# Attention scores over 128 contraction rows, and attention values with both split parts side by side, in one kernel

## The reference

```
xn = layernorm(x); q = (xn @ w_q) / 8; k, v = split(context @ w_kv)
scores = einsum('bqhd,bkhd->bhqk', q, k)          # 112 x 375 for each head
attn = softmax(scores, axis=-1)
out = einsum('bhqk,bkhd->bqhd', attn, v).reshape(B, SQ, 1024) @ w_out + b_out
x = x + tanh(g) * tanh(gate) * out
# then: Fourier mix, a one-head attention, a mixture of 16 experts (top 4), each with a layernorm ahead
```

## Time and profile before

| | |
|---|---|
| median of 3 runs | 1162.66 us (1161.47 to 1164.37) |
| the profiled execution | 1161.57 us |
| its span | 1159.8 us |
| outside the span | 1.8 us |
| PE busy | 1075.9 us, 93% |
| DVE busy | 773.1 us, 67% |
| ACT busy | 631.4 us, 54% |
| POOL busy | 519.8 us, 45% |
| mean granted TensorE clock | 0.984 |
| bytes moved by DMA | 95.8 MB |

### The profile page before, as it was taken

One profiled execution on the slowest core, in us unless ns is written; L12 is line 12 of the kernel. 1 busy time (PEld: TensorE's weight loads), 2 busy tenths in 40 slices (PEclk: granted clock), 3 DMA queues, 4 the chain that ended last, 5 costly groups with the idle time before them and its releaser, 6 DMA issues.

```text
span 1159.8 us, 22342 instructions
## 1 busy us (share of the span) xinstructions
PE 1075.9 (93%) x7361; PEld 930.8 (80%) x7361; DVE 773.1 (67%) x1963; ACT 631.4 (54%) x1676; POOL 519.8 (45%) x745
## 2 busy tenths in 40 slices
PE   3889999999999999999999999999999779899995
PEld 3688888888888888888788888888887668789983
DVE  2544677767676767776676777676766665686665
ACT  2533556555656565655556565656564545555650
POOL 3512345453535454454535354536354404565441
PEclk9989999999999999999999999999999888999998
DMA  5395882010101011010001010101000522234469
GB/s 150 96 329 207 309 297 63 5 34 9 30 27 31 27 31 35 23 35 22 23 16 32 8 38 9 31 9 31 5 18 9 176 83 78 99 108 152 133 198 287
DMA packets 82382, 95.82 MB, mean 83 GB/s; under 512 B 9291, under 2 KB 74445, under 8 KB 82272
## 3 DMA queue, kind: packets, MB, share of 16 engines
q1 hardware_dynamic: 41904, 44.94, 13.5%
q10 hardware_dynamic: 31520, 32.51, 7.9%
q0 software_dynamic: 8848, 16.96, 4.2%
HBM read 41.98 MB, written 52.39 MB: 81 GB/s over the span
## 4 chain that ended last, share of the span: by engine, by line
PE 61%; DVE 16%; ACT 10%; issue 6%; DMA 4%; POOL 3%; SPq 1%; DVEq 0%; ACTq 0%; POOLq 0%
PE ps_kv L1568 14%; PE ps_ot L1854 8%; PE ps_ot L1668 5%; PE ps_kv L1650 5%; PE ps_s L1811 5%; PE ps_pt L1821 5%; ACT prob L938 4%; DVE negmax L1467 3%; PE ps_pt L1780 3%; PE ps_ot L1793 3%; DVE pT_lo L1478 2%; DVE k_lo L1152 2%; ACT v_hi L928 2%; DMA zb<-places 2%; PE ps_ot L1712 2%
## 5 line engine op out<-in xcount | busy, mean ns | idle before, releaser
L855 POOL TENSOR_TENSOR prob<-prob,rinv 112x750 f32<-112x750 f32 x128 | 185.4, 1448 | 310.7 <-DVE rinv L1472 310.4
L938 ACT ACTIVATE prob<-ps_s,negmax 112x375 f32<-112x375 f32 x256 | 144.7, 570 | 236.4 <-DVE negmax L1467 236.4
L1478 DVE TENSOR_TENSOR pT_lo<-ps_pt,pT_hi 125x672 fp32r<-125x672 f32 x128 | 109.7, 857 | 77.0 <-ACT pT_hi L1051 77.0
L1568 PE MATMUL ps_kv<-ctxT_hi,wkv 128*128 128x376 f32 x512 | 141.6, 357 | 7.8 <-DVE v_lo L1156 3.8
L1467 DVE TENSOR_REDUCE negmax<-ps_s 112x2 f32<-112x750 f32 x128 | 119.0, 930 | 0.1
L1156 DVE TENSOR_TENSOR v_lo<-ps_kv,v_hi 125x512 fp32r<-125x512 f32 x96 | 66.4, 692 | 77.2 <-ACT v_hi L928 77.2
L1568 PE MATMUL ps_kv<-wkv,ctxT_hi 128*125 128x512 f32 x384 | 112.2, 414 | 3.6 <-DVE n_e L1116 2.3
L1821 PE MATMUL ps_pt<-ident,prob 112*125 112x112 f32 x768 | 104.9, 273 | 1.3 <-POOL prob L855 1.3
L814 POOL DMA_INDIRECT places<-ysb,place_i x72 | 70.3, 976 | 69.1 <-ACT ysb L1010 55.9
L1051 ACT ACTIVATE pT_hi<-ps_pt 125x672 fp32r<-125x672 f32 x128 | 93.5, 730 | 9.0 <-PE ps_pt L1821 1.0
L1821 PEld LDWEIGHTS ps_pt<-ident,prob 112*125 112x125 f32 x768 | 95.1, 191 | 1.7 <-POOL prob L855 1.7
(11 more groups left out here) (298 smaller groups left out, 2623.8 us busy)
## 6 DMA issues: line engine op xcount, KB each, us to landing
rows_by_expert<-stage_w ACTq DMA_DIRECT2D x16, 1920.0 KB, 7.3
xg<-rows_by_expert SPq DMA_DIRECT2D x72, 128.0 KB, 2.1
zb<-places SPq DMA_DIRECT2D x16, 448.0 KB, 15.0
arena<-in_L_ffn_mlp_w SPq DMA_DIRECT2D x24, 256.0 KB, 4.4
ctx_in<-in_ctx SPq DMA_DIRECT2D x16, 375.0 KB
acc<-in_L_xattn_w_kv SPq DMA_DIRECT2D x4, 512.0 KB, 13.1
stage_w<-in_L_ffn_mlp_w SPq DMA_DIRECT2D x8, 256.0 KB, 3.0
x_in<-in_x SPq DMA_DIRECT2D x16, 112.0 KB, 2.1
```

Source lines behind the costliest of these rows:

```text
L855: e_prob.done(eng.tensor_tensor(prob[0:TQ, p % 2, :, :], prob[0:TQ, p % 2, :, :], rinv[:, 2 * p:2 * p + 2].unsqueeze(2).broadcast_to([TQ, ...
L938: e_exp.done(eng.activation(prob[0:TQ, p % 2, half, :], S[0:TQ, half, 0:SK], ACT.Exp, bias=negmax[:, h:h + 1], accum_out=rowsum[:, h:h + 1]))
L1478: e_pt_lo.done(eng.tensor_tensor(pT_lo[:, :, :, :].rearrange("p h k t -> p h (k t)"), PT[0:KEYT, :, 0:NKEY * TQ], pT_hi[:, :, :, :].bitcas ...
L1568: last = eng.matmul(out_, lhs(i, k), rhs(j, k), start=(n == 1), stop=(n == KT * len(PASSES)))
```

## The change

Nothing else of the computation is changed; the three terms are the same.

- **Scores.** `kx` holds for each head hi keys on partitions 0 to 63 and lo keys on 64 to 127. `qx_hi` holds hi queries twice, on both halves; `qx_lo` holds lo queries on 0 to 63 and zeros on 64 to 127. S(p) is then four matmuls over 128 rows. ACT writes a pair's hi keys in two copies instead of one (the second moves head 1 from partitions 64 to 127 down to 0 to 63). DVE writes the lo keys to `k_low`, the lo queries to `q_nat`, and SP moves them into place with DMAs between two SBUF places: two for each pair's keys, six for each half of the queries, 28 a batch. S(p) waits for these DMAs instead of for DVE.
- **Values.** `vx` holds hi and lo values of one head side by side (128 columns), `pT` hi and lo probabilities side by side (224 columns). O(p) is six matmuls of 125x128 by 125x224, whose four quarters are the four products, of which lo x lo is not used. The three others are added outside PE: ACT copies one (64x224, `o_part`), DVE adds a second to it (64x224), waits for that, and adds the third in two instructions of 64x112 that write `oT`. These three are on DVE after `pT_lo` in every odd slot.
- **Order.** `KV_AT`: k2, v2 from slots 0, 1 to 1, 2; x from 10 to 9; c0, c1 from 12, 13 to 11, 12; q0 from 14 to 12; k0, k1 from 14, 15 to 13, 14. SP's loads are written by slot between the moves.
- **Room.** `acc` is gone, its uses go to `stage_w`; `TURN`, the order in which experts' weights are placed, and the filling with zeros follow from that.

```diff
-        KV_AT = (("k", 2, 0), ("v", 2, 1), ("k", 3, 3), ("q", 1, 4), ("k", 4, 5), ("v", 3, 6),
-                 ("k", 5, 7), ("v", 4, 8), ("k", 6, 9), ("v", 5, 10), ("k", 7, 11), ("x", 0, -6),
-                 ("c", 0, -4), ("c", 1, -3), ("q", 0, -2), ("k", 0, -2), ("k", 1, -1), ("v", 0, -1),
+        KV_AT = (("k", 2, 1), ("v", 2, 2), ("k", 3, 3), ("q", 1, 4), ("k", 4, 5), ("v", 3, 6),
+                 ("k", 5, 7), ("v", 4, 8), ("k", 6, 9), ("v", 5, 10), ("k", 7, 11), ("x", 0, -7),
+                 ("c", 0, -5), ("c", 1, -4), ("q", 0, -4), ("k", 0, -3), ("k", 1, -2), ("v", 0, -1),
                  ("v", 1, 0), ("r", 0, 36), ("e", 0, 38))
...
+                if kind == "k":
+                    for head in range(2):
+                        eng.dma_start(kx[64:128, n, head, :].bitcast(F32),
+                                      k_low[64 * head:64 * head + 64, n % 2, :].bitcast(F32)
+                                      ).then_inc(f_k[n % 2], 16)
...
-                        for half in range(2):
-                            rows_ = slice(64 * half, 64 * half + 64)
-                            last = eng.activation(oT[rows_, p, :], OT[rows_, half * TQ:(half + 1) * TQ],
-                                                  ACT.Copy)
-                        e_oT.done(last)
+                        e_part.done(eng.activation(o_part[:, :, :], O[64:128, :, 0, :], ACT.Copy))
...
-                    ins = eng.activation(k_hi[:, n, :], bank[:, 0:SKE], ACT.Copy)
+                    eng.activation(kx[:, n, 0, :], bank[:, 0:SKE], ACT.Copy)
+                    ins = eng.activation(kx[0:64, n, 1, :], bank[64:128, 0:SKE], ACT.Copy)
...
+                for p in range(NP):
+                    st = due(g, AT_O[p] + 1)
+                    if st:
+                        e_part.wait_ge(eng, st, p + 1)
+                        co(eng.tensor_tensor(o_part[:, :, :], O[0:64, :, 1, :], o_part[:, :, :], ALU.add))
+                        co.wait_ge()
+                        for half in range(2):
+                            last = eng.tensor_tensor(oT[64 * half:64 * half + 64, p, :], O[0:64, half, 0, :],
+                                                     o_part[:, half, :], ALU.add)
+                        e_oT.done(last)
...
-                        eng.wait_ge(kv_dve, KV_LO[max(use_of(st, "q", p // 4), use_of(st, "k", p)) + 1])
+                        eng.wait_ge(f_q, queries(st.off, p // 4) + Q_MOVES)
+                        eng.wait_ge(f_k[p % 2], keys(st.off, p) + K_MOVES)
                         e_exp.wait_ge(eng, st, 2 * p)
-                        for n, (i, j) in enumerate(PASSES):
-                            for half in range(2):
-                                rows_ = slice(64 * half, 64 * half + 64)
-                                last = eng.matmul(S[0:TQ, half, 0:SKE], qq[i][rows_, p, :],
-                                                  kk[j][rows_, p, :], start=(n == 0),
-                                                  stop=(n == len(PASSES) - 1))
+                        for half in range(2):
+                            for n in range(2):
+                                last = eng.matmul(S[0:TQ, half, 0:SKE], qx[n][:, half, p, :], kx[:, p, half, :],
+                                                  start=(n == 0), stop=(n == 1))
...
-                        n = 0
-                        for i, j in PASSES:
+                        for half in range(2):
                             for k in range(NKEY):
-                                n += 1
-                                last = eng.matmul(OT[:, 0:2 * TQ].rearrange("p (h t) -> p h t", t=TQ),
-                                                  vv[i][0:KEYT, k, p * 128:(p + 1) * 128],
-                                                  pT[j][:, :, k, :], start=(n == 1),
-                                                  stop=(n == NKEY * len(PASSES)))
+                                last = eng.matmul(OT[:, 2 * half * TQ:2 * (half + 1) * TQ],
+                                                  vx[0:KEYT, k, 2 * p + half, :, :].rearrange("p a d -> p (a d)"),
+                                                  pT[:, half, k, :, :].rearrange("p a t -> p (a t)"),
+                                                  start=(k == 0), stop=(k == NKEY - 1))
```

198 lines of the change are left out of this document (115 added, 83 removed).

## The result

The changed kernel takes 1321.67 us (median of 4 runs, 1317.43 to 1328.91) where the one before takes 1162.64: **1.137 times as long** (1.132 to 1.143). The forecast was 1232 and the range ended at 1275. The sign was right, the size was 90 us short. The profiled execution took 1321.24 us with a span of 1319.4. All that follows is in spans: +159.6 us.

A forecast was written before the change was run, and what follows sets the result against it. It took two paths of nearly one length, PE's and one through DVE and ACT, as the bound. 1161.6 + 63 (middle batches) + 6 (start) = 1230.6 profiled, 1232 for the median; range 1165 to 1275.

The forecast's parts named there:

- The six places: Where PE would stand longer in a batch: n12t, x, v5, c1, slots 0 to 3, out projection; 8.5 us together.
- the signs: What would show the forecast in a profile: PE's and DVE's busy times, named waits, n12t with 1.9 us instead of 0.5.
- Against 3.5 gained, a batch is 4.5 us longer: Waits of 8.5 us, less 0.5 for today's, against PE's gain: a batch of 59.3 us, +63 us over 14 batches.
- PE's gain: Fewer matmuls: 0.34 us a pair in O(p), 0.10 in the scores; 3.5 us a batch.
- Places 2 to 6: Longer PE waits: x 0.7 us, v5 1.4, c1 1.3, slots 0 to 3 2.0, out projection 1.7.
- S for the moves: Scores waiting for SP's DMAs of keys and queries; in the middle batches costed at nothing.
- The clock: Rival, clock or moves worse: granted clock 0.83 adds 5 us a batch, or 1300; chance of 1275 or more 0.11.
- DVE absorbs it: Rival: additions fall into DVE's 16 us of waiting a batch, PE is the bound; 1113 us, chance 0.12.
- The start: Moves of q1 and k4 behind slot 4's loads delay S(4) from 57.70 to 64 to 65 us; +6 us, between 0 and 11.
- They double the bytes but not the load at any one time: Claim about SP's six moves of queries, which hold SP for 2.5 us, with S two slots away.
- Half absorbed: Rival: places 2 to 5 cost half, DVE's part is 0.65; 1.5 us a batch, 1185 us, chance 0.17.

The follow-up runs named there:

- e6: The changed kernel without its three additions a pair: ACT copies the high parts' product, the two small products are left out; 1212.65 us, ratio 1.044.
- e11: The kernel before with the values' half alone, without any addition (small products computed but left out); 1135.28 us, ratio 0.978.
- e3: The kernel before with the changed `KV_AT` order alone; 1208.62 us, ratio 1.009.
- e9: The changed kernel with the block of additions moved ahead of `pT_lo`; 1261.1 us, ratio 1.085.
- e10: The kernel before with the values' half alone, its additions ahead of `pT_lo`; 1174.84 us, ratio 1.009.
- e7: The kernel before with three more additions a pair on DVE behind `pT_lo`, on a buffer nobody waits for; 1263.51 us, ratio 1.087.
- e4: The changed kernel with only 6 of the 15 blocks of each region zeroed; 1328.99 us, ratio 1.109.

## Why the prediction was wrong

**What was right.** PE busy at 93% was not read as the bound. PE's work a batch: forecast 50.3, measured 50.2 in e6. DVE's: 45.6 against 45.2. The additions: 0.87 us against 0.92. S with 128 rows gains next to nothing: e6 and e11 differ by 1.0 us of PE's work a batch where 0.8 was forecast. The six places all showed up; in the batch from 602.92 to 664.95 they are n12t 1.7 us (1.4 in the sum, 1.9 among the signs), c1 1.7 (1.3), out projection 1.9 (1.7), v5 1.6 (1.4), x 1.1 (0.7), slots 0 to 3 2.4 (2.0). Nearly every wait was named and priced within half a microsecond.

**The step that failed is the sum behind them**: "Against 3.5 gained, a batch is 4.5 us longer". It missed by 3.9 us a batch, 47 of the 90 us, in three terms:
- PE's gain was subtracted in full. At full clock PE's busy time fell from 53.8 to 51.2, by 2.6. The other 0.9 isn't work: e6 has the same matmuls in 50.2, with half as many waits. That it is what PE loses at each restart is argued, not shown.
- The waits grew by 9.8 us at full clock (62.03 less 51.22, against 1.0 before), not 8.0. Places 2 to 6 were each 0.2 to 0.4 short, and a wait of 0.4 in slot 7, of the keys for a lo part of values, was not on the list. S for the moves, costed at nothing in the middle, is none of it: it waits 1.0 to 1.2 us in four of the six batches at full clock, but all six take 62.0, since the wait for T9's layer norm or for oT(7) behind it is shorter by as much.
- The clock, in the forecast a rival with 0.11, came in half the batches: 1.1 us a batch on average. The reading of the earlier trace rows as a danger was right, its weight was not. The rival took the busy share of the whole batch (17 of 20) as its measure; what the falls follow here are single waits of 1.7 to 1.9 us, though the batches at full clock have the same waits without a fall.

The runs put another sum in its place (e11, e6): the values' half without additions gives back 1.6 us and not 2.7, the scores' half costs 2.2 us, of which the order is 1.6 (e3), and the additions cost 6.7 of their 7.3. "Against 3.5 gained" is what fails in it: shortening PE's work moved PE to its waits, and only a part of it shortened the batch. A shorter sum, 54.7 + 7.0 for the additions at full price = 61.7 us, comes near the measured 62.0, but by luck: it leaves out the order (+2.2 with the scores' half) and PE's gain (-1.6), which nearly cancel, and the additions' price depends on their place (e9, e10). I gave the opposite ("DVE absorbs it") 0.12 and half of it 0.17; e7 shows that even with nobody waiting for the sums, it doesn't absorb. DVE had its 16 idle microseconds, but the additions were put behind its waits (e9, e10).

**The start and the zeroing.** Forecast +6 and nothing; measured +22.2, and 17.8 in the two batches behind it beyond their 8.4 each. These are 42 of the 90 us missed. "With less zeroing beside them I take 64 to 65 us": S(4) came at 74.92. Wrong were the issue time, 0.32 us, where a move takes 0.60 in the middle and up to 3.5 beside the loads, and above all the landing time. I took 2.1, at most 3.9 us, from loads of x made beside little else, although had 15 us beside the same loads. The chain of waits of the changed kernel has it, beside the loads and then beside the zeroing:

```profile
138.37 8.49 DMA qx_lo<-q_nat
...
178.30 7.30 DMA qx_lo<-q_nat
...
213.70 9.01 DMA qx_lo<-q_nat
```

"They double the bytes but not the load at any one time" left out that the zeroing is such a load for two batches. e4 takes away three fifths of it and 20 us go.

**Two slips.** `n12t` stands at 1.4 us in the sum, from which 0.5 for today's waits is taken, and at 1.9 among the signs; if the 1.4 comes on top of today's 0.5, a batch was forecast 0.5 us too short by this alone. "Half absorbed" gave 1185, which leaves out the start: 1.5 us in 14 batches and the 6 us come to 1190.

**The range.** 1165 to 1275 took in half-absorbed cases and stopped short of the clock's. The terms that it held fixed (landing under load, gain in full) were the ones that moved, all to one side.
